# One indirect gather of a DLRM tower fetched by SyncE row by row; first back transposes, padding and first-layer evictions in other places

## What is computed

```python
e = jnp.stack([tbl_0[ids[:, 0]], ..., tbl_25[ids[:, 25]]], axis=1)     # 512 x 26 x 128
combined = jnp.concatenate([e, dense_x[:, None, :]], axis=1)           # 512 x 27 x 128
interact = jnp.einsum('bfd,bgd->bfg', combined, combined)
z = interact[:, _TRIU_I, _TRIU_J]                                      # 512 x 351
h = jnp.concatenate([z, dense_x], axis=1)                              # 512 x 479
h = jnp.maximum(h @ W_top1 + b_top1, 0.0)                              # 512 x 512
h = jnp.maximum(h @ W_top2 + b_top2, 0.0)                              # 512 x 256
y = h @ W_top3                                                         # 512 x 1
```

## Time and profile before

| | us |
|---|---|
| median of 3 runs | 108.18 (108.18 to 108.19) |
| the profiled execution | 108.26 |
| its span, first to last instruction | 106.4 |
| PE busy | 99.0 |
| DVE busy | 79.4 |
| ACT busy | 73.9 |
| POOL busy | 67.7 |

### The profile page before, as it was taken

How to read it: one execution, slowest core, us unless ns; L and a number is a source line. 1 busy time by engine, 2 the same in 40 slices (tenths; PEclk the granted TensorE clock), 3 DMA queues, 4 the chain that set the end, 5 groups by cost and what they waited for, 6 DMA issues and landing times.

```text
span 106.4 us, 2498 instructions
## 1 busy us (share of the span) xinstructions
PE 99.0 (93%) x998; PEld 78.6 (74%) x998; DVE 79.4 (75%) x141; ACT 73.9 (69%) x147; POOL 67.7 (64%) x72
## 2 busy tenths in 40 slices
PE   5999999999999999999989979889999985999991
PEld 1246765765686676789789967879999974899991
DVE  6899999999999999999758994951058712586120
ACT  4499999999999999999167772632257631374430
POOL 3777777777877778777777777777777773000000
PEclk9999999999999999999999999999999999999999
DMA  4861826655374654899122222111222211000000
GB/s 54 317 237 49 230 74 214 158 188 180 122 223 76 226 163 131 252 398 265 51 55 54 66 59 54 51 49 49 55 60 65 54 49 49 6 0 0 6 0 1
DMA packets 5239, 11.68 MB, mean 110 GB/s; under 512 B 1998, under 2 KB 2520, under 8 KB 5228
## 3 DMA queue, kind: packets, MB, share of 16 engines
q1 hardware_dynamic: 3160, 7.31, 21.6%
q0 software_dynamic: 2048, 4.20, 14.4%
q10 hardware_dynamic: 20, 0.02, 0.1%
HBM read 11.48 MB, written 0.00 MB: 108 GB/s over the span
## 4 chain that ended last, share of the span: by engine, by line
POOL 61%; issue 18%; PE 12%; DMA 4%; POOLq 1%; DVE 0%; ACT 0%
POOL rows L313 61%; PE gram_ps L670 3%; DMA rows<-table,ids_sb 2%; DMA ids_sb<-ids 2%; PE top_ps L737 2%; PE tr_ps L712 1%; POOLq L112 1%; PE act_ps L749 1%; PE dve_ps L749 1%; PE top_ps L762 1%; PE dve_ps L726 1%; PE dve_ps L712 1%; PE act_ps L712 1%; PE gram_ps L706 0%; PE tr_ps L683 0%
## 5 line engine op out<-in xcount | busy, mean ns | idle before, releaser
L313 POOL DMA_INDIRECT rows<-table,ids_sb x64 | 66.8, 1044 | 20.7 <-issue 19.2
L630 PE MATMUL gram_ps<-onehot,high 128*128 128x512 f32 x82 | 22.2, 405 | 0.1
L638 PE MATMUL gram_ps<-onehot,low 128*128 128x512 f32 x82 | 21.6, 406 | 0.0
L630 PEld LDWEIGHTS gram_ps<-onehot,high 128*128 128x128 f32 x82 | 14.5, 188 | 6.1 <-DVE onehot L483 2.8
L638 PEld LDWEIGHTS gram_ps<-onehot,low 128*128 128x128 f32 x82 | 14.5, 188 | 4.7 <-issue 1.8
L670 PE MATMUL gram_ps<-xt 128*58 128x52 f32 x512 | 15.1, 217 | 1.1 <-issue 1.1
L670 PEld LDWEIGHTS gram_ps<-xt 128*58 128x58 f32 x512 | 14.3, 133 | 2.0 <-issue 1.5
L483 DVE TENSOR_TENSOR onehot<-dve_ps,row_f 128x1536 fp32r<-128x1536 f32 (+1 forms) x10 | 15.2, 1524 | 0.0
L522 DVE COPY gram_sb<-gram_ps 26x208 f32<-26x208 f32 x32 | 12.0, 376 | 3.9 <-PE gram_ps L670 1.8
L483 DVE TENSOR_TENSOR onehot<-gram_ps,row_f 128x1024 fp32r<-128x1024 f32 (+1 forms) x10 | 14.8, 1478 | 0.0
L341 ACT ACTIVATE gram_sb<-gram_ps 26x208 f32<-26x208 f32 x32 | 10.7, 334 | 5.1 <-PE gram_ps L670 3.7
(11 more groups left out here) (99 smaller groups left out, 111.1 us busy)
## 6 DMA issues: line engine op xcount, KB each, us to landing
table<-table SPq DMA_DIRECT2D x9, 512.0 KB, 3.7
rows<-table,ids_sb POOLq DMA_INDIRECT x64, 2.9
w1p_sb<-w_pairs SPq DMA_DIRECT2D x1, 768.0 KB
table<-table SPq DMA_DIRECT2D x1, 640.0 KB
w_sb<-w SPq DMA_DIRECT2D x1, 512.0 KB
dense_sb<-dense SPq DMA_DIRECT2D x1, 256.0 KB, 5.8
w1d_sb<-w_dense SPq DMA_DIRECT2D x1, 256.0 KB
ids_sb<-ids SPq DMA_DIRECT2D x1, 52.0 KB, 2.0
```

Of the source, the lines that this page charges most:

```text
L313: pool.indirect_dma_start(rows[:, t, s - 1, :], None, tables[f], bass.IndirectOffsetOnAxis(ids_sb[:, t, f:f + 1], 0)).then_inc(gathered[t] ...
L630: pe.matmul(pick_ps[b][:], high[:, b, c, :], onehot[:, b, c, :], start=(c == 0), stop=False)
L638: last = pe.matmul(pick_ps[b][:], low[:, b, c, :], onehot[:, b, c, :], start=False, stop=(c == CHUNKS[o] - 1))
```

## The change

Four edits, with the line numbers of the new file where rows of the order show them:

1. The last gather (tile 3, slot 16) is left out of POOL's list. SP fetches its 128 rows one by one: a register is loaded from `row_ids` (the 128 ids in one line, a new input that SP loads after dense), and a transfer of one row (512 bytes) takes its source address from it. Ten of these stand ahead of table 2 and its wait, seven behind the issue of each table 2 to 9 (56), and the remaining 62 behind the loads of weights and biases.
2. The padding of tile 2 is written by ACT before its first one-hot, that of tile 3 by DVE behind the copy of dense into `xt`. `gram(0)` waits for all four.
3. `back` of tile 0 becomes `back_first`: its three transposes go to `top_ps`, one ACT copy takes them out, and they stand between the third and the fourth set of `gram(1)`, on PE and on ACT.
4. ACT's `first_layer` waits only for the parts that it copies, and `dense_part` waits for each bank of the first layer apart.

```diff
         @block.sync
         def _(sp):
             sp.dma_start(ids_sb[:], ids.rearrange("(p t) f -> p t f", t=TILES)).then_inc(ids_in, 16)
+            def rows_by_address(at):
+                f = SLOT_FIELD[LAST_SLOT]
+                for p in at:
+                    r = sp.value_load(row_ids[0:1, p:p + 1], min_val=0, max_val=tables[f].shape[0] - 1)
+                    sp.dma_start(rows[p:p + 1, TILES - 1, LAST_SLOT - 1, :], tables[f][bass.ds(r, 1)]
+                                 ).then_inc(gathered[TILES - 1][-1], 16)
             for o, f in enumerate(ONEHOT):
...
+                if o == TABLES:
+                    sp.wait_ge(row_ids_in, 16)
+                    rows_by_address(range(0, ROWS_FIRST))
                 if o >= TABLES:
                     sp.wait_ge(low_ready, REST * (o - TABLES + 1))
                 sp.dma_start(table[:, o % TABLES, 0:CHUNKS[o]], ...).then_inc(table_in[o % TABLES], 16)
                 if o == TABLES - 1:
                     sp.dma_start(dense_sb[:], ...).then_inc(dense_in, 16)
+                    sp.dma_start(row_ids[:], ids_in_line).then_inc(row_ids_in, 16)
+                if o >= TABLES:
+                    rows_by_address(range(ROWS_FIRST + (o - TABLES) * ROWS_A_TABLE, ROWS_FIRST + (o - TABLES + 1) * ROWS_A_TABLE))
                 if o == WEIGHTS_AFTER:
                     sp.dma_start(w1p_sb[:], w1_pairs).then_inc(weights_in, 16)
...
+            rows_by_address(range(ROWS_FIRST + (NO - TABLES) * ROWS_A_TABLE, P))
             sp.wait_ge(y_out, TILES)
...
                     for s in BANK_SLOTS[t][n]:
+                        if (t, s) == (TILES - 1, LAST_SLOT):
+                            continue
...
             def first_layer(n):
-                act.wait_ge(h1_ready, n * (N1 // P))
+                act.wait_ge(h1_ready, n * (N1 // P) - (1 if n == TILES - 1 else 2))
...
+            act.wait_ge(zeros_ready, 1)
+            act.activation(xt[:, 2, :, N_SLOTS:PAD], zeros ... , ACT.Copy).then_inc(pad_zero, 1)
             act.wait_ge(row_neg_ready, 1)
...
-            gram(1)
-            back(1)
+            gram(1, range(SETS - 1))
+            back_first()
+            gram(1, (SETS - 1,))
...
             dve.tensor_copy(xt[:, :, :, 0] ... ).then_inc(dense_out, 1)
+            dve.memset(xt[:, 3, :, N_SLOTS:PAD], 0.0).then_inc(pad_zero, 1)
...
-            dve.memset(xt[:, 2, :, N_SLOTS:PAD], 0.0).then_inc(pad_zero, 1)
             gram(1)
-            back(1)
             transposed(2, (0,))
-            dve.memset(xt[:, 3, :, N_SLOTS:PAD], 0.0).then_inc(pad_zero, 1)
...
-                    pe.wait_ge(gathered[t][n], 16 * len(slots))
+                    pe.wait_ge(gathered[t][n], 16 * (P if slots[-1] == LAST_SLOT and t == TILES - 1 else len(slots)))
...
             def dense_part(t, parts=range(N1 // P)):
-                if t:
-                    pe.wait_ge(h1_out_act, 2 * t)
-                    pe.wait_ge(h1_out_dve, 2 * t)
                 ps = h1_banks(t)
                 for m in parts:
+                    if t:
+                        pe.wait_ge((h1_out_act, h1_out_dve)[m // 2], 2 * t)
...
-            gram(1)
+            gram(1, range(SETS - 1))
+            back_first()
+            gram(1, (SETS - 1,))
             transposes(2, (0, 1))
-            back(0)
             first_layer(0, range(N1 // P))
```

More of the change, by code:

```diff
@@ L651, in transposes, with gram @@
                     last.then_inc(tr_ready, 1)
-            def gram(t):
+            def gram(t, sets=range(SETS)):
                 pe.wait_ge(tr_out_dve, TR_OUT[0][t + 1])
                 pe.wait_ge(tr_out_act, TR_OUT[1][t + 1])
-                for s in range(SETS):
+                for s in sets:
                     n = t * SETS + s
@@ L694, in back, with back_first @@
                                         packed[:, c * P:(c + 1) * P], ident[:])
+                last.then_inc(back_ready, 1)
+            def back_first():
+                pe.wait_ge(packed_act, 1)
+                pe.wait_ge(packed_dve, 1)
+                for c in range(NC):
+                    last = pe.transpose(top_ps[:, c, :], packed[:, c * P:(c + 1) * P], ident[:])
                 last.then_inc(back_ready, 1)
@@ L881 @@
     out = nc.dram_tensor("y", (B, 1), F32, kind="ExternalOutput").ap()
-    tower(nc, ap["dense"], ap["ids"], ap["ids_by_field"], [ap[f"table{f}"] for f in range(N_FIELDS)],
+    tower(nc, ap["dense"], ap["ids"], ap["ids_by_field"], ap["ids_in_line"], [ap[f"table{f}"] for f in range(N_FIELDS)],
           ap["w1_pairs"], ap["w1_dense"], ap["b1"], ap["w2"], ap["b2"], ap["w3"], out)
```

24 lines of the change are left out of this document (18 added, 6 removed).

## The result

| | before | after |
|---|---|---|
| median, us | 108.19 (108.18 to 108.19, 4 runs) | 197.26 (196.44 to 197.70, 4 runs) |
| after to before | | 1.822, interval 1.816 to 1.829 |
| profiled span, us | 106.4 | 195.8 |

The changed kernel takes 1.8 times as long. The forecast was 107.6 us. What holds is rival A: SP has become the bound.

A forecast was written before the change was run, and what follows sets the result against it. POOL's last gathers, then PE's remaining list, were taken to bound the kernel. Span 106.4 - 0.27 - 0.3 = 105.8, so 107.7 us profiled and 107.6 median; range 106.9 to 108.8, with rival A outside it.

The forecast's parts named there:

- rival A: SP becomes the bound once a row takes over 0.59 us: last row at 14.6 + 128r, 122 us or more; chance 0.20.
- What bounds the kernel: At the end of the span: POOL up to the last gathers, then PE's remaining list behind them.
- Part 1: One gather less on POOL removes only PE's wait for the 64th gather, 0.27 us.
- Part 2: SP's time for one row, r: taken as 0.52 us, between 0.33 and 1.6.
- The stall of table 2: Ten rows ahead of table 2 delay its transfer; ACT stalls about 1.5 us, 0.3 to 3 at other values.
- What the stall does to POOL: Gathers run freely during table 2's stall, shifting the 63rd by +0.25 to -1.0 us; mean taken, -0.3.
- The rule for one gather: A gather starting in L497, or up to 0.1 ahead, waits for its end, then takes 0.82 to 0.83 us.
- Part 3: Edits 3 and 4 remove PE waits of 0.48 and 0.43, 0.9 us, paying for the stall before bank 3.
- The rest at nothing: Paddings on ACT and DVE hidden behind waits for PE, later weights harmless: no cost; 0.59 us per padding if not hidden.

The follow-up runs named there:

- low_from_psum: Kernel before, but for tables 1 to 8 DVE's L497 subtraction is a PSUM copy of zeros, so part of the values is missing; 106.39 us.
- late_32_alone: Kernel before with 32 rows fetched by address behind the biases and 96 by one plain transfer, without edits 2 to 4; 108.68 us.
- loads_by_16: Changed kernel, but one register load brings 16 ids and the bounds test is left out; 107.13 us, ratio 1.000.
- by_16_strided: Changed kernel with 16 ids a load, no bounds test, ids read by a strided transfer, inputs of the kernel before; 108.20 us.
- by_16_strided_4: Changed kernel with 16 ids a load, no bounds test, strided ids, no additional input, 4 rows ahead of table 2 instead of 10; 107.11 us.
- no_rows: Changed kernel with the 64th gather back on POOL and no rows on SP; edits 2 to 4 and the additional input stay; 108.88 us.
- before_input: Kernel before with one additional input that nothing reads; 108.86 us, ratio 1.013.
- no_rows_no_input: Changed kernel with the 64th gather back on POOL, no rows on SP and no additional input; 108.18 us, ratio 1.000.

## Why the prediction was wrong, step by step

- **What bounds the kernel (right).** POOL's gathers up to bank 3, then PE's list. low_from_psum took away what stretches the gathers, and the time fell until PE's own list bound it.
- **Part 1, 0.27 (right in kind).** In late_32_alone, which has only this part, y_sb was written 0.41 earlier.
- **Part 2, r = 0.52 (the step that failed).** Measured 1.245. The bounds of 0.33 and 1.6 held it, but the choice did not. I argued from the size of what is loaded ("the load and the three register instructions move 4 bytes and no descriptors"). Size is the smaller part of the load's 0.49: 16 ids in one load take 1.23, not 16 times as much. The register instructions got no time of their own, though two of them are the bounds test that the code asks for (min_val and max_val in the load), 0.17 and with its gaps 0.29; nor did the gaps between the six instructions, 0.25 in all. The margin was seen and not weighed: the decision point was 0.59, each 0.01 beyond cost 1.3 us, and the range for r had four fifths of its width above it. The Trainium skill's floor for the load (DMA: Bandwidth & Descriptors, "Latency and other measured facts", some 600 ns) is a little high, as the median here was 488 ns and the shortest 432; but the r that it gave, 0.93, lay on the right side.
- **Rival A (right in mechanism, short in size).** 14.6 + 128 x 1.245 = 174.0 for the last row; PE got it at 176.8. By the rival's sum the time would be 191.5, measured 197.3. The profiled execution took 197.65, 6.1 more. Of these, 2.8 lie ahead of the last row: SP's last issue ended 3.9 later than the sum has it (the ids 0.2, the tables 0.7 at 0.41 each, the weights 0.2, the rest between the rows, 1.25 each in the mean and five or six pauses of 0.3), and the row landed 1.0 after it, not 2. The other 3.2 are the tail: half clock in gram(3) and ahead of it, and the store. 0.20 was too small a chance for it.
- **The stall of table 2 (right, given r).** row_ids landed at 7.22 (predicted 7.0); with r near 0.5 table 2 was issued at 12.18 (12.2), and ACT waited 1.58 for it in loads_by_16 (about 1.5).
- **What the stall does to POOL (right in kind, too small).** The shift was to lie between +0.25 and -1.0. From 86.77 (a gather less than before's 88.02), the last gather moved by -1.9 in loads_by_16 and by -2.8 in by_16_strided, where ACT waited 1.58 and 1.64 for table 2. But it moved by -2.6 in by_16_strided_4 too, without a wait for the table, and without a row on SP the 64th gather moved by -1.5 in no_rows and -1.3 in before_input (88.02 to 86.54 and 86.73). The rule for one gather was right; following it over thirty gathers, from a start that differs by 1 us between traces, was not.
- **Part 3 (right in kind, the size uncertain).** Edits 2 to 4 bring PE 1.16 earlier to bank 3 (the weight load's wait there is 2.53 in no_rows_no_input against 1.37 in the earlier trace rows, for a landing at the same 89.36, and the table stage ended alike), but by 0.4 behind the table stage in low_from_psum_edits; predicted 0.9. Both waits are gone in both. "Without the stall these edits would be worth nothing" held: no_rows_no_input, which has the edits and no rows on SP, took 108.18 against 108.19.
- **The rest at nothing.** The paddings were hidden in no_rows_no_input, where PE comes 1.16 earlier, no less than the two waits. The additional input was not free: 0.7 to 0.8 on the last store. The prediction had no term for it.

## What to carry to other kernels

Where a sum hangs on a price that no row shows, and the outcome tips inside its bounds, the forecast is a bet on that price: count the instructions of the compiled program and give each the shortest row that exists, gaps included, before choosing a value. Fetching rows by register address is a matter of the load: take many values in one, and leave the bounds test out where the data allow. Before taking work off an engine that waits in step with another, find out what keeps them in step; here that was worth more (1.8 us, in a kernel that leaves a part out) than the whole idea (1.1 at best). And where executions of one kernel go in steps, compare traces of two kernels only when they began alike: a difference of 1 us in the first 8 looks here just like the effect of rows ahead of a table.

## What the runs showed of the hardware

- A register load on SP took 0.49 us for one value and 1.23 for 16; the issue of a one-row transfer with an address from a register 0.23 to 0.27.
- A DVE subtraction of two SBUF operands (L497) holds up an indirect gather on GpSimd that starts within it, by up to 0.8 us; a copy from PSUM of the same length does not.
- The same program gives times in steps: the kernel before mostly near 106.6, 107.7 and 108.2 us, and 109.4 to 109.9 at a mean granted clock of 0.98. TensorE's pace on the same ten matmuls doubled at 4.95 us in one trace and at 7.45 in another (kernel before, no_rows). The later start can give the shorter run: with the rounding of table 2 at 15.1 to 15.2 in place of 14.15 and no rows on SP, the gathers lost 5.0 and 5.2 us to L497 in place of 6.5 (no_rows, before_input).
- In these traces TensorE waited 1.48 and 1.80 us ahead of bank 3 with no change in the granted clock behind it; after waits of 2.21, 2.26 and 2.29 us the rows show 0.50 (1.2 GHz), and after 24.75 and 47.16 too. In no_rows_no_input, behind the 2.29:

```profile
89.89 1.49 PE L755 MATMUL act_ps<-pairs_t,w1p_sb 128*128 128x128 f32 x6
```

- An input that nothing reads made the last store of 2 KB land in 2.0 us in place of 1.1. The cause is open: it goes with the set of inputs, by one trace of each kernel.
